# A softmax attention whose second query chunk takes its steps on the diagonal between its full steps

## The chip, the cores and the metric

The kernel runs on one core of a Trainium2 chip. The metric is the time of one execution on the device in microseconds. Five engines work side by side, each through its own list of instructions in order: TensorE (PE, with its weight loads as PEld), VectorE (DVE), ScalarE (ACT), GpSimd (POOL) and SyncE (SP, which issues DMAs). They meet only at semaphores.

## What is computed

Two transformer layers over x of 2 sequences, 1024 tokens and 256 channels. Layer 0 is a polynomial attention of 16 heads and an expert layer with two experts. Layer 1, cut to what matters here, is a causal softmax attention of 32 heads of width 8, followed by an expert layer with 32 experts:

```python
scores = jnp.einsum('bhqd,bhkd->bhqk', q, k) / math.sqrt(dh)
causal = jnp.tril(jnp.ones((T, T), dtype=bool))
scores = jnp.where(causal[None, None], scores, -jnp.inf)
weights = jax.nn.softmax(scores, axis=-1)
out = jnp.einsum('bhqk,bhkd->bhqd', weights, v)
```

Nothing outside this softmax attention is touched.

## The kernel before, in words

The softmax attention works through 16 quads, G = 0 to 15: four heads of one sequence each, eight quads per sequence. A planner (`plan_second_attention`) writes the order of the work once; every engine then takes its own part of it in that order.

A quad has two chunks of 512 queries. `key_steps(c)` (line 308) lists the steps of chunk c; a step is one block of 128 keys, or two such blocks packed into one width:

- chunk 0: step 0 is key block 0, 512 queries wide; step 1 packs key blocks 3 (128 wide) and 1 (384 wide); step 2 is key block 2, 256 wide. All three lie on the diagonal.
- chunk 1: steps 0 to 3 are key blocks 0 to 3, each 512 wide and wholly under the diagonal ("full"). Step 4 is key block 4, 512 wide, on the diagonal; step 5 packs key blocks 7 (128) and 5 (384); step 6 is key block 6, 256 wide.

So a quad has ten steps, and each step has two halves of two heads. One half is, in PE's order (`weights`, line 1175, and `weigh`, line 1152):

1. in quads 8 to 15 (`KEPT_BUSY`), one matmul of constants that is never read (`keep_busy`, L2450);
2. the scores of two heads (`scores`, L2436), into a pair of PSUM banks;
3. beside them a unit of score maxima of the other two heads of the *next* quad (L2408), into two of three single banks. DVE reduces them (L3059 with a mask, L3062 without). A table, `PLAN_OF_STEP`, says at which of the ten places n = 0 to 9 such a unit stands; only n = 5 has none. The last quad has none at all;
4. one part of a `weigh` (L2461): the products of the softmax weights with v, accumulated in one bank. They belong to the step two places earlier (`weigh_due`, line 1170, with `WEIGHTS_AHEAD = 2`). A full step has two parts of 256 columns; step 5 has parts of 384 and 128; step 6 has two parts of 128. At the first places of a quad they are held back and then come three in a row.

ACT takes the exponentials of each half (L2790), 1024 elements per partition, or 512 for a 256-wide step. For a step on the diagonal POOL then clears the forbidden triangle (`mask_weights`, L3716), once for each key block of the step, and the weigh of that step waits for it. After the last weigh of a chunk ("closes") ACT copies the bank out (L2709, `o_cols`).

Other work stands at fractional places in a list called `between`. For every quad: `cut_max` and `turn_max` of the second half at 0 and 2 (POOL's copies L367 and L3673, PE's transposes L2347, ACT's copy to `qt`); `normalize` of the previous quad at 2.5 (PE transposes the output, DVE takes the reciprocal at L3088 and multiplies at L3091 into `ao`, which frees a pair of banks); `cut` of quad G + 2 on POOL at 3.5 (at 4.2 in quad 6); `turn` of quad G + 2 at 7.2. In quads 5 and 6 the projection of the second sequence runs in between, in quads 8 and 9 a `norm` of four tiles stands at place 6 and 4 (POOL, L3681 to L3707), and from quad 13 on POOL issues scatter DMAs for the next layer.

The order of the ten steps before is chunk 0, steps 0 to 2, then chunk 1, steps 0 to 6. The loop that walks them is line 1328:

```python
for n, (c, step) in enumerate((c, step) for c in range(SEQ // QCH) for step in range(len(key_steps(c)))):
    half_steps = weights(G, c, step, beside[2 * n:2 * n + 2])
```

Of the kernel before, what the change touches and what calls it, by code (L numbers as in the profile page):

```python
# [17 lines left out]
BATCH, SEQ, CH = 2, 1024, 256  # L18
# [5 lines left out]
QCH = 512  # L24
# [283 lines left out]
def key_steps(c):  # L308


    d = 4 * c
    return [([(key, 0)], QCH) for key in range(d + 1)] + [([(d + 3, 3 * P), (d + 1, 0)], QCH), ([(d + 2, 0)], 2 * P)]
# [5 lines left out]

RAISED_ON_ACT = ((1, 1, 2), (1, 2, 2), (1, 3, 0))
MIXED_STEPS = ((0, 0), (1, 0), (0, 1), (0, 2), (1, 1), (1, 4), (1, 5), (1, 2), (1, 6), (1, 3))  # L320


CUT_PLACES = (((2.5, 3, 3.5, 4, 5, 7.5), (4.5, 5, 7.6, 7.7, 8, 9.9)), ((0, 1, 2, 2.0, 4, 6.5), (4, 4.5, 6.6, 6.7, 7.5, 9.5)))
# [46 lines left out]
def build_program(nc, ins, out):  # L370
    ctx = ExitStack()
    with ctx:
# [115 lines left out]
        def walk(work_of):  # L488
# [501 lines left out]
            def plan_second_attention(A, start, late, w_ready, during, tail, amid):  # L990
# [160 lines left out]
                def weigh():  # L1151
                    G, c, step, part, slot, ready = due.pop(0)
                    b, quad = divmod(G, quads)
                    bank_free = o_free[0] if step == 0 and part == 0 else ()
                    done = mark(weighed, L, b, quad, c, step, part)
                    if part:
                        probs_ring.give(slot, done)
                    closes, oc, oc_free = part and step == len(key_steps(c)) - 1, None, ()
                    out_open[0] = None if closes else False
                    if closes:  # L1160
                        if c == 0:
                            o_turn[G] = (*oc_ring.take(), [])
                        oc, oc_free = o_turn[G][0:2]
                        o_out = mark(act_copied, "o", L, b, quad, c)
                        o_turn[G][2].append(o_out)
                        o_free[0] = (o_out,)
                    do("weigh", A=A, b=b, quad=quad, c=c, step=step, part=part, slot=slot, waits=(*ready, *bank_free),
                       first=step == 0 and part == 0, closes=closes, oc=oc, oc_free=oc_free)
# [6 lines left out]
                def weights(G, c, step, maxima):  # L1175
                    b, quad = divmod(G, quads)
                    keys, _ = key_steps(c)[step]
                    p_slot, p_free = probs_ring.take()
                    ready = []
                    for h0 in (0, 2):  # L1180
                        slot, slot_free = pairs.take()
                        q_slot, _, q_ready = qt_at["max", G]
                        k_slot, _, k_ready = kt_at[G]
                        gone = mark(scored, L, b, quad, c, step, h0)
                        done = mark(exped, L, b, quad, c, step, h0)
                        pairs.give(slot, done)
                        ready.append(done)
                        if c == 1 and step == len(key_steps(c)) - 1 and h0:
                            kt_ring.give(k_slot, gone)
                            max_ring.give(q_slot, gone)  # L1190
                        units = maxima[h0 // 2]
                        if G in KEPT_BUSY:
                            keep_busy(1)
                        do("scores", A=A, b=b, quad=quad, c=c, step=step, h0=h0, p_slot=p_slot, p_free=p_free, slot=slot,
                           slot_free=slot_free, q_slot=2 + q_slot, k_slot=k_slot, rows_ready=(q_ready[c], *k_ready),
                           qk_done=(), on_act=False, before=start, maxima=max_places(*units[0]) if units else None)
                        for unit in units[1:]:
                            max_unit(unit[0], unit[1:])
                        weigh_due(h0 // 2)
                        if h0 == 0:  # L1200
                            yield
                    if keys[0][0] >= 4 * c:
                        for key, _ in keys:
                            masked = mark(pool_raised, L, b, quad, c, step, "masked", key)
                        do("mask_weights", A=A, b=b, quad=quad, c=c, step=step, p_slot=p_slot, ready=tuple(ready))
                        ready = [masked]
                    due.extend((G, c, step, part, p_slot, tuple(ready)) for part in range(2))
# [78 lines left out]
                for G in range(last + 1):  # L1286
                    b, quad = divmod(G, quads)
                    between = list(during(b, quad))
                    beside = [[] for _ in range(2 * len(PLAN_OF_STEP))]
                    if G == 0:  # L1290
                        for n, unit in enumerate(max_units(LATER_PLANS)):
                            beside[n // 2].append((0, *unit))
                        for n, unit in enumerate(max_units()):
                            beside[6 + (n // 2 if n < 8 else n - 4)].append((1, *unit))
                        between += [(1.5, lambda: turn(1)), (2.8, lambda: cut_max(0, 1)), (2.9, lambda: turn_max(0, 1)),
                                    (5, lambda: cut_max(1, 0)), (8, lambda: turn_max(1, 0)), (0.5, scales[0]), (1.4, scales[1])]
                    else:
                        between += [(0, lambda: cut_max(G, 1)), (2, lambda: turn_max(G, 1))]
                    if 0 < G < last:
                        for n, plan in enumerate(PLAN_OF_STEP):  # L1300
                            if plan is not None:
                                for half in range(2):
                                    beside[2 * n + half].append((G + 1, plan, 2 - 2 * half))
                        between += [(2.8, lambda: cut_max(G + 1, 0)), (5, lambda: turn_max(G + 1, 0))]
                    if G + 2 <= last:
                        at = {quads - 3: 2.6, quads - 2: 4.2}.get(G, 3.5)
                        between += [(at, lambda: cut(G + 2)), (7.2, lambda: turn(G + 2))]
                    if quad:
                        between.append((2.5, lambda: normalize(G - 1)))
                    elif b:  # L1310
                        between += [(1, lambda: normalize_half(0, 1)), (2, lambda: turn_out(0, 1, 0)), (2.8, lambda: turn_out(0, 1, 1)),
                                    (3.8, lambda: project_out(0, 1)),
                                    (6, norm)]
                    if (b, quad) == (1, 1):
                        between.append((4, norm))
                    if G == quads - 3:
                        between += [(1.2 + 1.1 * n, lambda n=n: bring_half_x(1, n // 2, n % 2)) for n in range(4)]
                        between += [(5.4 + 0.9 * t, lambda t=t: project(1, t)) for t in range(5)]
                    if G == quads - 2:
                        between += [(0.6 + 1.1 * (t - 5), lambda t=t: project(1, t)) for t in range(5, TILES)]  # L1320
                    if quad == quads - 1:
                        between += [(5, lambda: normalize_half(1, 0)), (5.8, lambda: turn_out(1, 0, 0)), (6.2, lambda: turn_out(1, 0, 1)),
                                    (7, lambda: project_out(1, 0)),
                                    (7.1, lambda: early.extend(plan_norm(norms_due.pop(0)))), (7.5, lambda: early[0]()),
                                    (9, lambda: early[1]()), (9.1, lambda: early[2]())] if b else [
                                    (5.5, lambda: normalize_half(0, 0)), (6.8, lambda: turn_out(0, 0, 0)), (7.6, lambda: turn_out(0, 0, 1)), (8.5, lambda: project_out(0, 0))]
                    between.sort(key=lambda p: p[0])
                    for n, (c, step) in enumerate((c, step) for c in range(SEQ // QCH) for step in range(len(key_steps(c)))):
                        half_steps = weights(G, c, step, beside[2 * n:2 * n + 2])
                        for at in (n, n + 0.5):  # L1330
                            while between and between[0][0] <= at:
                                between.pop(0)[1]()
                            next(half_steps, None)
                    for _, what in between:
                        what()
# [2537 lines left out]
```

How the kernel before makes its waits and increments, by code:

```python
    def wait_ge(self, signal, *name):  # L83
        value = signal.at[name]
        if self.reached.get(signal.sem, 0) < value:
            self.eng.wait_ge(signal.sem, value)
            self.reached[signal.sem] = value
# [2139 lines left out]
            def attention_weights(A, free):  # L2227
                L = A.layer
                for e in free:
                    q.wait_ge(*e)
                load(f"wqkv{L}", stage[:, 0:KB * 3 * CH].rearrange("p (k n) -> p k n", k=KB),
                     ins[f"wqkv{L}"].rearrange("(k p) n -> p k n", p=P))
                load(f"wo{L}", stage[:, KB * 3 * CH:KB * 4 * CH].rearrange("p (k n) -> p k n", k=KB),
                     ins[f"wo{L}"].rearrange("(k p) n -> p k n", p=P))
                if L == 0:
                    load_x(1)
# [1 line left out]
            def attention_setup(A, start):  # L2238
                L = A.layer
                for e in start:
                    q.wait_ge(*e)
                load(f"cos{L}", A.cos[:], ins[f"cos{L}"])
                load(f"sin{L}", A.sin[:], ins[f"sin{L}"])
                if not A.softmax:
                    load("qk_scale", A.qk_scale[:], ins["ln_scale"].partition_broadcast(P))
                    load("qk_bias", A.qk_bias[:], ins["ln_bias"].partition_broadcast(P))
# [8 lines left out]
            def many_setup(start):  # L2255
                for e in start:
                    q.wait_ge(*e)
                load(f"gw{ml}", M.gw[:], ins["router1"].rearrange("(k p) n -> p k n", p=P))
```

## Time and profile before

| what | us |
| --- | --- |
| median of 3 runs | 1542.97 |
| lowest, highest | 1540.48, 1550.19 |
| the profiled execution's own time | 1543.04 |
| its span, from the first to the last instruction | 1541.3 |
| the softmax attention in it, first to last exponential | 645.7 to 1246.4 |

The span is what the rows of the trace add up to; about 1.7 us lie outside it. Rows of a timeline give start and duration in us, and in brackets the idle time of the engine just before and what ended it. TensorE's clock is given as the share of full speed that was granted: 1.00 is 2.4 GHz, 0.50 is 1.2 GHz.

### The profile page before, as it was taken

The page shows a single profiled execution, that of the slowest core. Times are in us where ns is not written, and L with a number is a line of the kernel's source. Part 1 is how long each engine was busy: PE and PEld are TensorE (multiplying, and loading weights), DVE is VectorE, ACT ScalarE, POOL GpSimd, SP SyncE. Part 2 cuts the span into 40 slices and gives each one's busy share as a digit, 9 for nine tenths or more (in the row PEclk, how much of TensorE's full clock was granted, in tenths as well). Part 3 has the DMA queues.
Part 4 walks back from the last instruction along what each step waited for, and adds up shares of the span by engine and source line. Part 5 has one row for each costly group of instructions (what it writes and reads, how often), then busy time and mean ns, then how long its engine had stood idle before and what let it go on. Part 6 is the DMA issues. An engine that isn't in the chain of part 4 may idle for free.

```text
span 1541.3 us, 26468 instructions
## 1 busy us (share of the span) xinstructions
PE 1305.7 (85%) x9434; PEld 827.6 (54%) x9434; DVE 1041.7 (68%) x2748; ACT 880.1 (57%) x1245; POOL 681.1 (44%) x862
## 2 busy tenths in 40 slices
PE   6477756776789999689999998999999988899995
PEld 4233443342567877444544554434444454899984
DVE  7757787768444365878877477767997366555685
ACT  3578626877343342347777566666667652466660
POOL 7477254647202103313232741442237637766661
PEclk9599986988999999769999989979999979999999
DMA  2690000012302101000000000000004435677876
GB/s 95 217 362 29 1 1 1 1 42 99 110 11 72 42 11 36 11 1 1 2 1 1 1 1 1 1 2 1 1 2 159 175 148 198 216 210 215 265 259 225
DMA packets 69143, 124.40 MB, mean 81 GB/s; under 512 B 7318, under 2 KB 55190, under 8 KB 67992
## 3 DMA queue, kind: packets, MB, share of 16 engines
q1 hardware_dynamic: 56728, 85.99, 17.2%
q0 software_dynamic: 12288, 36.72, 6.4%
q8 instruction: 80, 1.31, 0.3%
q14 instruction: 47, 0.39, 0.1%
HBM read 60.29 MB, written 62.39 MB: 80 GB/s over the span
## 4 chain that ended last, share of the span: by engine, by line
PE 54%; DVE 25%; ACT 11%; POOL 4%; issue 4%; DMA 2%; SPq 0%; POOLq 0%; DVEq 0%; ACTq 0%
PE psum L2461 10%; PE psum L2347 8%; PE psum L2436 6%; PE psum L2667 6%; DVE psum L3059 5%; PE psum L2566 4%; DVE probs L3079 4%; ACT probs L2792 3%; PE psum L2690 3%; PE psum L2408 3%; PE psum L2587 3%; PE psum L362 2%; PE psum L2450 2%; DVE neg_max L3062 2%; PE psum L2368 2%
## 5 line engine op out<-in xcount | busy, mean ns | idle before, releaser
L2790 ACT ACTIVATE probs<-psum,exp_shift 128x1024 f32<-128x1024 f32 (+1 forms) x320 | 325.8, 1032 | 148.7 <-PE psum L2436 144.2
L3059 DVE CUSTOM_DVE_ANT_0 psum<-psum,stage 128x512 f32<-128x512 f32 (+3 forms) x512 | 288.6, 618 | 86.4 <-PE psum L2408 86.2
L3716 POOL TENSOR_SCALAR_AFFINE_SELECT probs<-probs 128x512 f32<-128x512 f32 x192 | 139.8, 740 | 370.9 <-ACT probs L2790 266.3
L2436 PE MATMUL psum<-qt,kt 32*128 32x512 f32 (+5 forms) x1152 | 240.7, 452 | 51.7 <-ACT probs L2792 18.8
L2408 PE MATMUL psum<-kt,qt 32*128 32x512 f32 (+3 forms) x768 | 209.3, 456 | 20.8 <-DVE neg_max L3059 14.4
L3079 DVE TENSOR_TENSOR probs<-probs 128x1024 f32<-128x1024 f32 (+1 forms) x136 | 170.2, 1296 | 61.6 <-ACT probs L2792 61.3
L2436 PEld LDWEIGHTS psum<-qt,kt 32*128 32x128 f32 (+1 forms) x1152 | 106.7, 197 | 193.7 <-issue 75.1
L2461 PE MATMUL psum<-probs,v 128*32 128x256 f32 (+3 forms) x2048 | 178.2, 447 | 1.9 <-POOL probs L3716 1.9
L3787 POOL DMA_INDIRECT results<-sp_y,sp_row x128 | 126.1, 985 | 57.4 <-ACT sp_y L2851 29.2
L2792 ACT ACTIVATE probs<-psum 128x1024 f32<-128x1024 f32 (+1 forms) x160 | 140.2, 946 | 5.8 <-PE psum L2436 5.8
L3062 DVE TENSOR_REDUCE neg_max<-psum 128x1 f32<-128x256 f32 (+3 forms) x256 | 111.1, 484 | 29.8 <-PE psum L2408 29.5
L2408 PEld LDWEIGHTS psum<-kt,qt 32*128 32x128 f32 x768 | 97.4, 198 | 51.4 <-DVE neg_max L3059 32.3
L3780 POOL DMA_INDIRECT many_x<-rows,where x96 | 93.0, 969 | 56.3 <-issue 19.5
L2347 PE MATMUL psum<-ident,q_rows 128*128 128x128 f32 x384 | 65.7, 313 | 52.5 <-ACT k_rows L2709 26.6
L2461 PE MATMUL psum<-probs,stage 128*32 128x256 f32 (+2 forms) x1280 | 99.9, 398 | 0.0
L2566 PE MATMUL psum<-sp_w,sp_xt 128*128 x512 | 95.2, 329 | 1.9 <-ACT sp_y L2851 1.0
L2566 PEld LDWEIGHTS psum<-sp_w,sp_xt 128*128 128x128 f32 x512 | 87.2, 192 | 6.9 <-issue 3.9
L2347 PEld LDWEIGHTS psum<-ident,q_rows 128*128 128x128 f32 x384 | 47.1, 157 | 75.8 <-DVE q_rows L3036 36.6
L2461 PEld LDWEIGHTS psum<-probs,v 128*32 128x32 f32 x2048 | 48.9, 114 | 65.8 <-issue 49.5
L2709 ACT ACTIVATE qt<-psum 128x512 fp32r<-128x512 f32 (+1 forms) x69 | 52.7, 764 | 44.0 <-PE psum L2347 43.9
L3059 DVE DVE_READ_ACCUMULATOR2_ANT neg_max<- 128x1 f32 x512 | 72.5, 142 | 0.0
L3513 DVE TENSOR_TENSOR shid<-psum,ssilu 128x512 f32<-128x512 f32 x36 | 24.9, 692 | 68.7 <-PE psum L2667 63.4
(362 smaller groups left out, 2587.0 us busy)
## 6 DMA issues: line engine op xcount, KB each, us to landing
many_x<-blank SPq DMA_DIRECT2D x2, 10240.0 KB, 50.6
sp_xs<-many_x SPq DMA_DIRECT2D x64, 320.0 KB, 3.8
sp_w<-in_sparse SPq DMA_DIRECT2D x8, 1280.0 KB, 9.2
x_turned<-results SPq DMA_DIRECT2D x8, 768.0 KB, 7.2
sp_back<-results SPq DMA_DIRECT2D x8, 768.0 KB, 10.5
sorted_x<-blank SPq DMA_DIRECT2D x2, 1152.0 KB, 6.5
sorted_y<-y SPq DMA_DIRECT2D x18, 128.0 KB, 1.7
rows<-in_x SPq DMA_DIRECT2D x4, 512.0 KB, 6.9
```

The costliest lines, as they stand in the source:

```text
L2347: inst = pe.transpose(dst[:, i * P:(i + 1) * P], tile, ident[:])
L2408: scored_max[i] = pe.matmul(psum[:, base:base + (k1 - k0) * P], A.qt[rows, q_slot, tile * P:(tile + 1) * P], A.kt[rows, k_slot, k0 * P:k1 ...
L2436: inst = pe.matmul(psum[:, base - early:base + QCH - q0], A.kt[rows, k_slot, key * P:(key + 1) * P], A.qt[rows, q_slot, c * QCH + q0 - ear ...
L2461: inst = pe.matmul(psum[32 * h:32 * h + 32, bank + q0:bank + q1], A.v_of(b)[:, key, col:col + 32], A.probs[:, slot, h, at:at + q1 - q0], s ...
L2566: inst = pe.matmul(psum[:, at:at + GATED], M.xt[:, x_slot, n * CH + k * P:n * CH + (k + 1) * P], M.w[:, bass.ds(which[2 * p + n], 1), k * ...
L2790: inst = act.activation(dst, view, ACT.Exp, bias=exp_shift[:, 0:1])
L2792: inst = act.activation(dst, view, ACT.Square)
L3059: inst = dve.tensor_tensor_reduce(src, src, causal_bf[:, (4 - cols) * P:4 * P], -1.0, -MASKED, ALU.add, ALU.min, dst)
L3062: inst = dve.tensor_reduce(dst, src, X_AXIS, ALU.max, negate=True)
L3079: dve.tensor_tensor(dst, dst, dst, ALU.mult).then_inc(raised.by(A.layer, b, quad, c, step, h0), 1)
L3716: pool.affine_select(out=dst, in_=dst, compare_op=ALU.is_ge, fill=0.0, base=0, pattern=[[0, 4], [1, P]], channel_multiplier=-1).then_inc(p ...
L3787: pool.indirect_dma_start(results, bass.IndirectOffsetOnAxis(M.row[:, row_slot, n:n + 1], 0), M.y[:, y_slot, n * CH:(n + 1) * CH], None).t ...
```

## The change

The ten steps of a quad are taken from a table in which chunk 1 alternates: 0, 4, 1, 5, 2, 6, 3. "The last step of a chunk", which decides when the output bank is closed and when the buffers of a quad are given back, now comes from the same table.

```diff
+EVEN_STEPS = ((0, 0), (0, 1), (0, 2), (1, 0), (1, 4), (1, 1), (1, 5), (1, 2), (1, 6), (1, 3))
+LAST_STEP = {c: [step for chunk, step in EVEN_STEPS if chunk == c][-1] for c in range(SEQ // QCH)}
...
-                    closes, oc, oc_free = part and step == len(key_steps(c)) - 1, None, ()
+                    closes, oc, oc_free = part and step == LAST_STEP[c], None, ()
...
-                        if c == 1 and step == len(key_steps(c)) - 1 and h0:
+                        if c == 1 and step == LAST_STEP[c] and h0:
...
-                    for n, (c, step) in enumerate((c, step) for c in range(SEQ // QCH) for step in range(len(key_steps(c)))):
+                    for n, (c, step) in enumerate(EVEN_STEPS):
```

The units of maxima and the list `between` go by the place n and stay where they are. What stands at the places is:

| n | 0 | 1 | 2 | 3 | 4 | 5 | 6 | 7 | 8 | 9 |
| --- | --- | --- | --- | --- | --- | --- | --- | --- | --- | --- |
| before | 0.0 | 0.1 | 0.2 | 1.0 | 1.1 | 1.2 | 1.3 | 1.4 | 1.5 | 1.6 |
| after | 0.0 | 0.1 | 0.2 | 1.0 | 1.4 | 1.1 | 1.5 | 1.2 | 1.6 | 1.3 |

All line numbers below line 330 are four higher in the changed kernel.

TensorE, from place n = 9 of one quad to n = 1 of the next (here quads 2 and 3), before. L2436 are scores, L2408 maxima, L2461 weighs, L2347 the transposes of `turn_max`:

```order
L2436 MATMUL psum<-qt,kt 128x256 x2
L2408 MATMUL psum<-kt,qt 128x512 x2
L2461 MATMUL psum<-probs,v 32x256 x4
L2436 MATMUL psum<-qt,kt 128x512 x2
L2408 MATMUL psum<-kt,qt 128x512 x2
L2461 MATMUL psum<-probs,v 32x384 x4
...
L2436 MATMUL psum<-qt,kt 128x384 x2
L2408 MATMUL psum<-kt,qt 128x128 x2
L2408 MATMUL psum<-kt,qt 128x384 x2
L2461 MATMUL psum<-probs,v 32x128 x4
L2347 MATMUL psum<-ident,q_rows 128x128 x4
```

and now:

```order
L2440 MATMUL psum<-qt,kt 128x512 x2
L2412 MATMUL psum<-kt,qt 128x512 x2
L2465 MATMUL psum<-probs,v 32x256 x4
L2440 MATMUL psum<-qt,kt 128x512 x2
L2412 MATMUL psum<-kt,qt 128x512 x2
L2465 MATMUL psum<-probs,v 32x128 x4
...
L2440 MATMUL psum<-qt,kt 128x384 x2
L2412 MATMUL psum<-kt,qt 128x128 x2
L2412 MATMUL psum<-kt,qt 128x384 x2
L2465 MATMUL psum<-probs,v 32x256 x4
L2351 MATMUL psum<-ident,q_rows 128x128 x4
```

The scores at n = 9 went from 256 to 512 columns, the first weigh of the next quad from 384 to 128, and the two weighs at n = 1, the second of which closes the chunk, from 128 to 256.

GpSimd in quad 8, from the last copy of `cut` over the `norm` to the next `cut_max`, before. L3716 are masks, L3681 to L3707 the `norm`:

```order
L367 TENSOR_SCALAR k_rows<-qk 128x32x8
L3681 TENSOR_TENSOR ln_stats<-ln_sd,ln_rstd 128x4
...
L3707 TENSOR_SCALAR rows<-rows,ln_mean_var,ln_rstd 128x256 x4
L3716 AFFINE_SELECT probs<-probs 128x4x128 x4
L367 TENSOR_SCALAR q_rows<-neg_max 128x16
```

and now:

```order
L371 TENSOR_SCALAR k_rows<-qk 128x32x8
L3720 AFFINE_SELECT probs<-probs 128x4x128
L3685 TENSOR_TENSOR ln_stats<-ln_sd,ln_rstd 128x4
...
L3711 TENSOR_SCALAR rows<-rows,ln_mean_var,ln_rstd 128x256 x4
L3720 AFFINE_SELECT probs<-probs 128x4x128 x3
L371 TENSOR_SCALAR q_rows<-neg_max 128x16
```

One mask went ahead of the `norm`. The number of masks is the same; the first of the three behind the `norm` is now that of place n = 6 and no longer that of n = 8.

## Rows read from the trace of the kernel before

**Rows 1.** groups by form: count | busy us, mean ns | idle

```profile
L2790 ACT ACTIVATE probs<-psum,exp_shift 128x1024 f32<-128x1024 f32 x256 | 281.9, 1118 | 115.2 <-PE psum L2436 111.5
...
L3059 DVE CUSTOM_DVE_ANT_0 psum<-psum,stage 128x512 f32<-128x512 f32 x316 | 209.7, 721 | 79.5 <-PE psum L2408 79.3
...
L3716 POOL TENSOR_SCALAR_AFFINE_SELECT probs<-probs 128x512 f32<-128x512 f32 x128 | 80.2, 639 | 266.6 <-ACT probs L2790 266.3
...
L2450 PE MATMUL psum<-stage 128*128 128x512 bf16 x126 | 50.9, 404 | 0.0
...
L2790 ACT ACTIVATE probs<-psum,exp_shift 128x512 f32<-128x512 f32 x64 | 43.9, 688 | 33.5 <-PE psum L2436 32.7
```

**Rows 2.** windows: PE PEld DVE ACT POOL, clock; quads 1-4, 1-15

```profile
701.60:731.50 29.90, 28.61 (x292) 14.10 (x288) 24.98 (x85) 23.56 (x27) 9.78 (x25) 1.00 0.01 1
731.50:761.30 29.80, 28.50 (x292) 14.11 (x288) 24.92 (x83) 23.56 (x27) 9.16 (x19) 1.00 0.01 2
761.30:794.60 33.30, 32.78 (x292) 16.03 (x288) 25.27 (x84) 23.79 (x27) 9.15 (x19) 0.85 0.01 1
794.60:824.40 29.80, 28.49 (x292) 14.10 (x288) 24.92 (x83) 23.57 (x27) 9.16 (x19) 1.00 0.00 1
701.60:1246.00 544.40, 511.37 (x4654) 250.82 (x4647) 394.30 (x1294) 375.88 (x423) 219.34 (x380) 0.94 0.07 26
```

**Rows 3.** timeline, TensorE, quad 2, places 0, 1, 3 and 5

```profile
731.27 0.85 PE L2461 MATMUL psum<-probs,v 128*32 128x384 f32 x8
...
732.06 0.49 PE L2436 MATMUL psum<-qt,kt 32*128 32x512 f32 x2
...
735.56 0.42 PE L2461 MATMUL psum<-probs,v 128*32 128x128 f32 x8
...
735.91 0.66 PE L2347 MATMUL psum<-ident,q_rows 128*128 128x128 f32 x4
...
739.39 0.50 PE L2436 MATMUL psum<-qt,kt 32*128 32x512 f32 x2 [0.54 <-DVE ao L3091]
...
747.67 0.64 PE L2461 MATMUL psum<-probs,v 128*32 128x256 f32 x8
...
748.24 0.50 PE L2436 MATMUL psum<-qt,kt 32*128 32x512 f32 x2
```

**Rows 4.** timeline, VectorE, quad 2: normalize, and the maxima after place 7

```profile
738.53 0.35 DVE L3088 RECIPROCAL o_rcp<-psum 128x32 f32<-128x32 f32 x1
...
754.69 0.70 DVE L3059 CUSTOM_DVE_ANT_0 psum<-psum,stage 128x512 f32<-128x512 f32 x1 [1.88 <-PE psum L2408]
```

**Rows 5.** windows around half-clock stretches, quads 3 and 7

```profile
761.30:765.80 4.50, 4.48 (x52) 2.02 (x44) 4.48 (x20) 3.83 (x4) 1.09 (x3) 0.98 0.00 0
765.80:775.80 10.00, 9.77 (x60) 5.14 (x56) 6.20 (x24) 3.76 (x6) 5.01 (x11) 0.50 0.00 0
915.80:926.00 10.20, 9.97 (x66) 5.21 (x64) 6.69 (x26) 4.37 (x6) 4.53 (x11) 0.50 0.01 2
```

**Rows 6.** timeline, GpSimd (quads 2, 6, 8, 9), then TensorE (quads 6, 8, 9)

```profile
744.86 0.41 POOL L367 TENSOR_SCALAR k_rows<-qk 128x256 fp32r<-128x256 f32 x1
...
899.22 0.41 POOL L367 TENSOR_SCALAR k_rows<-qk 128x256 fp32r<-128x256 f32 x1
...
982.30 4.86 POOL L3707 TENSOR_SCALAR rows<-rows,ln_mean_var,ln_rstd 128x256 f32<-128x256 f32 x4
...
1013.37 4.85 POOL L3707 TENSOR_SCALAR rows<-rows,ln_mean_var,ln_rstd 128x256 f32<-128x256 f32 x4
...
899.16 0.64 PE L2461 MATMUL psum<-probs,v 128*32 128x256 f32 x8
...
986.96 0.64 PE L2461 MATMUL psum<-probs,stage 128*32 128x256 f32 x8
...
1018.43 1.08 PE L2461 MATMUL psum<-probs,stage 128*32 128x256 f32 x8
```

**Rows 7.** timeline, ScalarE, last exponential of quad 15

```profile
1245.74 0.69 ACT L2790 ACTIVATE probs<-psum,exp_shift 128x512 f32<-128x512 f32 x1
```

## The prediction

> **What bounds the kernel now.** Only the softmax attention changes, so I read that stretch. First the groups by form [rows 1], for what one instruction costs. A unit of maxima is two reductions of 512 columns; DVE gives 209.7 us to 316 of them, 0.66 us each, so a unit takes 1.33 us. An exponential of a half takes ACT 1.12 us, or 0.69 us where the step is 256 wide; a mask takes POOL 0.64 us.
>
> Second the busy time in windows of one quad [rows 2]. Quads 1, 2 and 4 take 29.8 to 29.9 us each at a clock of 1.00. In 29.8 us PE is busy 28.5, DVE 24.9, ACT 23.6, POOL 9.2. No engine is full: PE's busy time holds its waits for banks inside matmuls, and DVE is idle for 29.8 - 24.9 = 4.9 us. Quad 3 does the same work, 292 matmuls, in 33.3 us at a clock of 0.85. That is the largest difference between equal quads, and this change could touch it.
>
> Third the timelines of PE and DVE in quad 2. Start to start, a weigh of 384 columns takes PE 732.06 - 731.27 = 0.79 us, one of 128 takes 735.91 - 735.56 = 0.35, one of 256 takes 748.24 - 747.67 = 0.57 [rows 3]. Scores with maxima beside them take about 0.43 us (the matmul of 0.50 without its tail). So a full half costs PE 0.43 + 0.57 = 1.0 us against DVE's 1.33: wherever maxima stand in a row, DVE sets the pace. It waits for PE where PE does other things: the row at 754.69 has DVE idle for 1.88 us behind the transposes of place 7 [rows 4]. From there DVE works on to place 3 of the next quad, where PE waits for DVE's `ao` [rows 3, 4].
>
> **The change part by part.** It adds and removes no instruction and no DMA. Ten steps keep ten places; the steps on the diagonal of chunk 1 move from places 7, 8, 9 to 4, 6, 8, and each weigh follows two places later. The sum of the work of each engine is the same, so only what it meets counts.
>
> 1. *Weighs, quads 1 to 7.* The weighs at the eight halves of n = 8, 9, 0, 1 were 256, 256, 256, 256, 384, 128, 128, 128. They become 384, 128, 256, 256, 128, 128, 256, 256. At n = 8 PE then needs 0.43 + 0.79 = 1.22 us, still under DVE's 1.33: nothing. At n = 1 each weigh costs 0.57 - 0.35 = 0.22 us more. The first stands before a wait for a bank of DVE and is lost in it. The second pushes the transposes at 735.91, ACT's copy and `normalize`, whose reciprocal at 738.53 DVE reaches with next to nothing to spare [rows 4], and PE waits for its product at 739.39 [rows 3]. I take half of 0.22, 0.1 us. The packed step at n = 6 costs PE 0.05 us more ahead of maxima. 0.15 x 7 = +1.0 us (bounds 0 and 0.22 x 7 = 1.5).
>
> 2. *Weighs, quads 8 to 14.* Here each half has one more matmul, of 0.40 us with its tail [rows 1] and some 0.32 without. The first half of n = 0 took PE 0.32 + 0.43 + 0.79 = 1.54 us, over DVE's 1.33; it now takes 1.1, and n = 1 with 1.32 stays under DVE's longer units of 128 and 384 there. The gain is at most 1.54 - 1.33 = 0.2 a quad. I take 0.15: -1.0 us (bounds 0 and -1.5).
>
> 3. *Masks behind other work on POOL.* A mask now stands at n = 4, behind `cut`, and its weigh is due at n = 6. In most quads the mask has room: in quad 2 `cut` ends at 744.86 + 0.41 = 745.27 [rows 6], and the weigh stands 0.43 us behind the scores of 748.24 [rows 3]. Three places are tight [rows 6]. Quad 6: `cut` ends at 899.22 + 0.41 = 899.63, the mask 0.64 and a hand-over later at 900.35; the weigh stood at 899.16: 1.2 us late. Quad 8: the `norm` ends at 982.30 + 4.86 = 987.16, the two masks of n = 6 at 988.4; the weigh at n = 8 stood at 986.96: 1.4 us late. Quad 9: the `norm` ends at 1018.22, the mask at 1018.95; the weigh stood at 1018.43: 0.5 us. Queued behind the weigh on PE are the next scores and maxima, for which ACT and DVE wait. The sum is 3.1 us if nothing hides it, 0 if DVE's backlog hides all of it; there is little backlog at n = 6, so I take 3.1.
>
> 4. *The end.* The last step of quad 15 had an exponential of 0.69 us (at 1245.74) [rows 7], a mask of 0.64 and two weighs of 128; now two exponentials of 1.12, no mask and two weighs of 256. ACT gains one short exponential at n = 8 and gives two at n = 9: +0.43; the closing weighs +0.44; the mask ended just ahead of its weigh and frees some 0.2. +0.7 us (bounds 0 and +1.3, all of it exposed).
>
> 5. *The clock.* In quad 3 the clock fell to half (1.2 GHz) from 765.8 to 775.8 [rows 5]; in quad 7 from 915.8 to 926.0, at the same place of the quad, from the end of n = 1 to n = 4. Before the first fall PE had not been idle (4.48 of 4.50 us busy), but had just done the three weighs of 128 columns in a row, with the narrow maxima of n = 1. These are the weighs that the change makes 256 wide. The price of a fall is 33.3 - 29.8 = 3.5 us [rows 2]. If the thin work brought the clock down, both go: -7.0 us. The other falls in the stretch (0.06 x 544.4 x 2 = 65 us at half clock in all, 20 of them these two) I leave. Bounds: 0, and 65 x 0.35 = -23, all gone at 3.5 us per 10. I take -7.0, since the row right before the fall is the one that changes.
>
> The Trainium skill ("TensorE: Matmul & The Clock Gate", section "HAM oscillation — how this bites in real kernels") speaks against term 5: it lays a fall of the clock to gaps in which the engine stands idle. The row before the fall shows no such gap. By that rule the change would give no clock back, and the sum would be 7 us higher, which is the first rival.
>
> Sum on the span of 1541.3: +1.0 - 1.0 + 3.1 + 0.7 - 7.0 = -3.2, so 1538.1; with the 1.7 us outside it 1539.8. The profiled execution took 1543.04 and the median is 1542.97, so this stands for the median too. About 1% (15 us) is what a measurement of this kernel can tell from no change.
>
> **The rivals.**
>
> *The clock stays as it is.* The falls do not hang on the width of two weighs. For it: quads 1, 2 and 4 have the same thin weighs and no fall. Against: two falls at one place. Time: 1539.8 + 7.0 = 1546.8.
>
> *Slower: the thin place only moves.* At n = 8 to n = 0 the weighs were 256, 256, 256, 256, 384, 128 and are 384, 128, 256, 256, 128, 128: four thin halves where there was one. If the clock falls there in the plain quads 1 to 7, each costs 3.5 us. All seven: 1546.8 + 24.5 = 1571. It decides over 1% from the fourth fall: 1546.8 + 14 = 1561, over 1558.4. For it: POOL's and PE's new waits in quads 6, 8 and 9 add idle time too. Against: scores are 512 wide at n = 9 now and not 256, and n = 1 is fuller by 0.44 us.
>
> *Faster: the clock stays up nearly everywhere.* More even weighs keep it up in the other quads as well. Time: 1546.8 - 23 = 1524. For it: term 5 claims less than a third of the 65 us at half clock. Against: nothing in the change touches the other waits of the stretch.
>
> *It does nothing.* Terms 1 to 5 within a microsecond or two, 1543; it lies inside the first two cases and has no chance of its own.
>
> **How the numbers follow.** My case 0.5 (from 1535 to 1544), the clock stays 0.28 (1543 to 1551), the thin place moves 0.10 (three in four of it over 1558), the clock stays up 0.12 (most of it under 1527.5). Faster by over 1%: 0.11. Slower by over 1%: 0.07. Within 1%: 0.82. The range leaves out the far ends of the last two cases: 1527 to 1554.
>
> **What would show it.** Right: 29.9 to 30.1 us for quads 1 to 4 each, quad 3 among them, with a clock of 1.00; the first weigh after place 6 in quad 6 and after place 8 in quad 8 with an idle time of over 1 us put to the masks (POOL); the last chunk closed within 1 us of before, against the start of quad 15. Wrong: a quad 3 at 33 us, or falls in quads 1, 2 or 4 between n = 8 and n = 1; DVE idle inside n = 8 to n = 3; PE waiting for masks in quads where I have them early. If a plain quad at full clock is over 0.5 us longer or shorter than 29.8, terms 1 and 2 are wrong, and the time follows that, sixteen times.

## The result, and the profile after

The changed kernel takes 1550.78 us (median of 20 runs, 1542.23 to 1574.58) beside 1542.83 of the kernel before (20 runs, 1532.48 to 1550.57). The ratio is 1.005, with a 95% interval of 1.0029 to 1.0072: 7.7 us slower by the ratio (8.0 between the medians), where 3 us faster was forecast. The runs spread more than before: 11 of the 20 are over 1550 us. The time goes with the clock: the two runs at a mean clock of 0.914 took 1543.0 and 1543.2 us, the three at 0.904 took 1551.4 to 1559.1. The profile caught a short run (1544.30 us, span 1542.5, clock 0.913), so it shows what the change costs at a good clock, and not the whole loss. Every ratio leaves out the runs that are over 1.5% above the fastest of their kernel, and the tables of profiles leave out two such runs (e3 and e15).

The windows of the quads after, to be held against [rows 2], from a quad's first exponential to the next one's (quads 1 to 5, 8, 9, 14, 15, then 1 to 15). The columns are as there: length, busy PE, PEld, DVE, ACT, POOL, then the clock:

```profile
701.60:732.90 31.30, 29.67 (x289) 14.13 (x288) 25.43 (x85) 23.76 (x27) 9.15 (x19) 0.95 0.00 1
732.90:764.60 31.70, 30.12 (x289) 14.21 (x288) 25.10 (x84) 23.60 (x27) 9.14 (x19) 0.95 0.01 2
764.60:794.60 30.00, 28.45 (x289) 13.91 (x288) 25.04 (x84) 23.55 (x26) 9.16 (x19) 1.00 0.00 1
794.60:824.70 30.10, 28.53 (x289) 13.89 (x288) 25.13 (x84) 23.62 (x27) 9.16 (x19) 1.00 0.00 1
824.70:876.00 51.30, 46.51 (x377) 26.58 (x376) 28.42 (x88) 30.01 (x40) 25.74 (x38) 0.90 0.00 1
954.30:997.30 43.00, 39.67 (x342) 19.96 (x340) 30.01 (x98) 25.43 (x28) 16.04 (x33) 0.88 0.00 1
997.30:1037.70 40.40, 36.22 (x309) 15.89 (x311) 27.68 (x95) 24.27 (x26) 16.03 (x33) 0.83 0.00 1
1176.00:1206.10 30.10, 28.73 (x290) 12.46 (x294) 25.50 (x85) 22.27 (x25) 23.44 (x30) 1.00 0.51 187
1206.10:1245.80 39.70, 36.75 (x292) 17.81 (x291) 10.20 (x35) 28.39 (x31) 23.91 (x29) 1.00 0.46 166
701.60:1245.80 544.20, 506.86 (x4654) 248.11 (x4654) 394.21 (x1296) 374.80 (x422) 219.16 (x375) 0.95 0.07 26
```

Quads 3 and 4 at a clock of 1.00 take 30.0 and 30.1 us, where quads 2 and 4 took 29.8. The fall of quad 3 is gone, as forecast. But quads 1 and 2 now each have a short stretch at half clock (0.95), quad 5 has 0.90 where it had none, and quad 8 has 0.88 where it had 0.96; quad 9 is low in both (0.83, and 0.79 before). Over all, the clock is 0.95 beside 0.94 and the 15 quads take 544.2 us beside 544.4. What was given back in one place was taken in another.

The waits for masks came where step 3 put them (TensorE's timeline in quads 6, 8 and 9, to be held against [rows 6]; behind the bracket is the idle time before the row and what ended it):

```profile
904.22 0.64 PE L2465 MATMUL psum<-probs,v 128*32 128x256 f32 x8 [1.10 <-POOL probs L3720]
...
991.68 0.85 PE L2465 MATMUL psum<-probs,stage 128*32 128x384 f32 x8 [1.25 <-POOL probs L3720]
...
1021.52 1.08 PE L2465 MATMUL psum<-probs,stage 128*32 128x256 f32 x8 [1.17 <-POOL probs L3720]
```

1.10 + 1.25 + 1.17 = 3.5 us, 3.1 forecast (1.2, 1.4 and 0.5: the one of quad 9 is twice what was taken). Of the weighs, the two rows that moved most are in TensorE's timeline at n = 0 and 1 of quad 3:

```profile
765.84 0.50 PE L2412 MATMUL psum<-kt,qt 32*128 32x512 f32 x1 [0.24 <-DVE neg_max L3063]
...
767.62 0.64 PE L2465 MATMUL psum<-probs,v 128*32 128x256 f32 x8
```

The first is a maxima matmul that waits 0.24 us for a bank of DVE (in quad 2 of before the pair at this place, from 732.06, took 0.81 us and had its wait inside); the second a weigh of 256 columns where [rows 3] has one of 128. And at the end, the transposes of `ranks` wait 2.41 us for ACT and waited 1.99.

### The profile page after: what moved, and what is told of

Same layout as the page of the kernel before. It is cut to its first block, busy times and chain, and to the rows that moved or that the text cites. A ratio compares the mean times of both kernels' runs of the same rounds, so it can differ in the third digit from the quotient of the medians.

```text
span 1542.5 us, 26467 instructions
## 1 busy us (share of the span) xinstructions
PE 1305.4 (85%) x9434; PEld 828.1 (54%) x9434; DVE 1041.4 (68%) x2748; ACT 879.1 (57%) x1245; POOL 681.0 (44%) x862
## 3 DMA queue, kind: packets, MB, share of 16 engines
q1 hardware_dynamic: 56728, 85.99, 17.1%
## 4 chain that ended last, share of the span: by engine, by line
PE 50%; DVE 26%; ACT 11%; POOL 5%; issue 4%; DMA 3%; SPq 0%; POOLq 0%; DVEq 0%; ACTq 0%
PE psum L2465 9%; PE psum L2351 8%; DVE psum L3063 7%; PE psum L2671 6%; PE psum L2440 5%; PE psum L2570 4%; DVE probs L3083 4%; ACT probs L2796 3%; PE psum L2694 3%; PE psum L2412 3%; PE psum L2591 3%; PE psum L366 2%; DVE neg_max L3066 2%; PE psum L2454 2%; PE psum L2372 2%
## 5 line engine op out<-in xcount | busy, mean ns | idle before, releaser
L3791 POOL DMA_INDIRECT results<-sp_y,sp_row x128 | 126.0, 984 | 55.8 <-ACT sp_y L2855 26.9
```

The lines of the kernel that those rows point to most:

```text
L3791: pool.indirect_dma_start(results, bass.IndirectOffsetOnAxis(M.row[:, row_slot, n:n + 1], 0), M.y[:, y_slot, n * CH:(n + 1) * CH], None).t ...
```

## The experiments

Each was timed in 5 rounds (e5 in 2) beside runs of the kernel before on the same chip, and the ratios are to those. Beside the first twelve the kernel before takes 1622.7 to 1624.6 us ("the 1623 runs"), beside the last six 1543.1 to 1544.5, as in the case. What makes the difference is not known: the record has chip 15 in both groups. The longer time lies from quad 14 on, where the scatter DMAs run: from the start of the last exponential 368 us remain in e1's profile and 297 in the one above. Quads 1 to 13 take the same in both groups. All edits but e5's stand on the changed kernel; a table says for each quad which order it takes:

```diff
+PLAIN_STEPS = ((0, 0), (0, 1), (0, 2), (1, 0), (1, 1), (1, 2), (1, 3), (1, 4), (1, 5), (1, 6))
+STEPS_OF = [EVEN_STEPS if G in (...) else PLAIN_STEPS for G in range(16)]
```

"New order" is EVEN_STEPS and "old order" PLAIN_STEPS.

**e1**, the changed kernel once more.

> The changed kernel once more, unchanged, to see whether a profile of its longer runs differs from the one at 1544.3 us by the clock alone. If the loss is made of falls of the clock, the median is again 5 to 9 us over the kernel before, the runs spread over 15 us or more, and a run's span follows its mean clock: over 1550 us at 0.905 and below, about 1543 at 0.912 and above. If it is made of fixed work (waits for masks, wider weighs), the runs spread no more than those of the kernel before (10 us or so) at one clock.

1.0111 (1.0071 to 1.015), 18 us, where 5 to 9 were expected. Clock against time holds: one run took 1652.2 us at 0.879, another 1627.9 at 0.898, and the runs spread over 30 us. Its quads 1 to 13 agree with those of the profile above to 0.1 us each, falls included.

**e2, e3, e4**: the change in three parts.

> The new order in quads 0 to 5 alone. Theory C (the thin place between n = 8 and n = 0 brings the clock down in the plain quads, which have no keep_busy): most of the loss is here, +5 to +8 us, with half-clock stretches in quads 1, 2 and 5. Theory M (the loss is in the places where PE waits for a mask): none of these is here, so +0 to +1.5 us (0.3 a quad) minus up to 3.5 for the fall of quad 3, so -2 to +1.5.

> The new order only in quads 6, 8 and 9, where PE waits for masks. Theory M: the waits of 1.10, 1.25 and 1.17 us and the clock that they cost are here: +4 to +8 us, with a half-clock stretch in each of quads 8 and 9. Theory C: the waits alone, +3 to +3.5 us, and the clock as before.

> The new order in quads 7 and 10 to 15. These have keep_busy (but for quad 7) and no mask that is late. Both theories: +0 to +1 us from the end of quad 15 and -0 to -3.5 from the fall of quad 7, so -3 to +1; the clock as in the kernel before. More than +3 here would break both and leave the order's own cost in the busy quads.

1.0024 (0.9992 to 1.0056), 1.004 (1.0001 to 1.0078) and 1.0078 (1.004 to 1.0115). The largest part is the one in which neither theory had a loss, so both are broken there. E2 and e3 decide nothing: 3.9 and 6.5 us, each with an interval of 5 to 6 us either way. E4's profile and e1's differ from the others in the last quads. E1 first, quads 14 and 15:

```profile
1179.60:1216.00 36.40, 30.82 (x285) 13.32 (x294) 25.93 (x86) 22.45 (x24) 24.75 (x33) 0.92 0.44 161
1216.00:1271.40 55.40, 52.44 (x288) 25.06 (x293) 10.08 (x32) 28.59 (x31) 22.37 (x26) 0.62 0.32 115
```

The clock falls at 1213.6, just ahead of quad 15, and stays at half for 44.4 us. Some 3 us before it, DVE starts a reduction 1.5 us after its matmul has ended, and PE stands still behind it (DVE's timeline, then TensorE's):

```profile
1210.85 0.70 DVE L3063 CUSTOM_DVE_ANT_0 psum<-psum,stage 128x512 f32<-128x512 f32 x1 [1.63 <-PE psum L2412]
```

```profile
1211.66 0.49 PE L2412 MATMUL psum<-kt,qt 32*128 32x512 f32 x1 [1.18 <-issue]
```

**e5**: the kernel before, unchanged, in the first group.

> The kernel before, unchanged, for a profile from the same chip as the runs beside it. If the loss of the changed kernel on the longer runs sits in its last quads (a stretch at half clock of 44 to 58 us from quad 14 on, seen in the two earlier runs with the new order there), this one has there less than 30 us at half clock; if it is the chip and not the order, it has as much.

0.9989 (0.9957 to 1.0021): no difference, as it must be. Quads 1, 2 and 15:

```profile
704.70:735.80 31.10, 30.07 (x289) 15.19 (x288) 25.37 (x85) 23.73 (x26) 10.14 (x28) 0.95 0.00 1
735.80:769.10 33.30, 32.77 (x289) 16.04 (x288) 25.25 (x84) 23.79 (x26) 9.15 (x20) 0.85 0.01 2
1209.50:1263.20 53.70, 49.75 (x288) 23.32 (x286) 11.34 (x33) 28.98 (x32) 23.40 (x29) 0.68 0.35 121
```

34.1 us at half clock in quad 15, 41 with quad 14: neither "less than 30" nor quite "as much". It begins 16 us into quad 15 and not before it. The first two rows tell more: in this execution of the same kernel the long fall is in quad 2, and quad 3 takes 29.9 us at 1.00. In which quad a fall stands is no property of the quad.

**e6, e7**: `KEPT_BUSY = tuple(range(1, 16))`, with the old and the new order.

> The old order with keep_busy in quads 1 to 15 in place of 8 to 15. Quads 1, 2 and 4 at full clock stay within 1 us of 29.8. Theory C (thin PE work before the fall): the falls of quads 3, 5 and 7 go, 3.5 us each: -5 to -14 us. If keep_busy costs more than it gives: 0 to +7.

> The new order with keep_busy in quads 1 to 15. Theory C (the loss of the new order is its thin place in the quads without keep_busy): this is within 3 us of e6, the old order with the same keep_busy. Theory M (masks that are late in quads 6, 8 and 9) or a loss in the last quads: it stays 5 to 15 us longer than e6.

1.008 (1.0044 to 1.0116) and 1.0156 (1.0121 to 1.0192). Quad 1 of e6:

```profile
706.70:738.30 31.60, 29.25 (x304) 14.03 (x309) 25.53 (x85) 24.12 (x26) 9.82 (x26) 1.00 0.00 1
```

The mean clock rises (0.898 in e6's runs, 0.894 beside them), but every plain quad pays 1.8 us at full clock, while a fall costs 3.5 in about one plain quad of four. E7 is 0.76% of the time behind e6, 12 us, which theory C excluded.

**e8**: the new order, with the mask ahead of what it waited for.

```diff
-                        at = {quads - 3: 2.6, quads - 2: 4.2}.get(G, 3.5)
+                        at = {quads - 3: 2.6, quads - 2: 4.6}.get(G, 3.5)
...
-                                    (6, norm)]
+                                    (6.6, norm)]
...
-                        between.append((4, norm))
+                        between.append((4.6, norm))
```

> The new order, with the norms of quads 8 and 9 and the cut of quad 6 moved half a step later, behind the mask that stood behind them. The waits of PE for masks in quads 6, 8 and 9 (1.10, 1.25, 1.17 us) go. Theory M: 4 to 8 us less than the changed kernel, quads 8 and 9 near 39.8 and 40.1 us as before. Theory C or a loss in the last quads: 3.5 us less and no more, still 5 us or more over the kernel before.

1.0041 (1.0 to 1.0082), where e1 had 1.0111: 11 us less, known to about 9. Quads 8 and 9:

```profile
959.50:999.30 39.80, 35.94 (x329) 18.98 (x334) 29.62 (x95) 25.53 (x29) 15.39 (x32) 0.96 0.01 1
999.30:1032.60 33.30, 29.43 (x305) 14.09 (x308) 27.77 (x94) 24.02 (x26) 16.48 (x34) 1.00 0.00 1
```

Together 73.1 us, and 83.4 in e1. PE's waits for masks in quads 6 to 9 fell to 1.5 us, from the 3.5 above; the rest of the ten is clock, 1.00 in quad 9 and not 0.83. Theory M has its 4 to 8 us and more in size. Its mechanism is not borne out: in the profile after, the falls of quads 8 and 9 begin 6.4 and 18.0 us into them (at 960.7 and 1015.3), and PE's waits for masks in these quads end later, at 991.7 and 1021.5. What brings those falls on, and why they go when the `norm` moves, isn't shown.

**e9, e10**: the new order in all quads but 14, and in 14 alone.

> The new order in every quad but 14, whose last weighs stand at the start of quad 15. Theory L (the loss is that the clock falls at the start of quad 15 and not 17 us later in it, because quad 14 ends thinner in the new order): the half-clock stretch in quad 15 begins 15 to 18 us after its first exponential, quads 14 and 15 together take 79 to 88 us and not 92 to 97, and the kernel is 6 to 10 us under the changed kernel of the same chips (about 1.005 times the kernel before). Theory S (the loss is spread over all quads): under 2 us less than the changed kernel.

> The new order in quad 14 alone. Theory L: +6 to +10 us over the kernel before, with a stretch at half clock that begins within 3 us of quad 15's first exponential; quads 1 to 13 as before. Theory S: under +1.5 us.

1.0035 (0.9993 to 1.0076) and 1.005 (1.0025 to 1.0076): theory L in both, for the 1623 runs. Quads 14 and 15 of e10:

```profile
1177.60:1214.80 37.20, 31.15 (x285) 13.55 (x294) 25.83 (x86) 22.31 (x25) 25.37 (x34) 0.89 0.42 156
1214.80:1273.00 58.20, 54.56 (x287) 25.27 (x290) 10.46 (x32) 29.20 (x31) 22.07 (x27) 0.60 0.30 111
```

95.4 us, and in e9 79.0. Over the profiles of the 1623 runs, the two last quads took 91.8, 97.1, 93.3, 91.8, 95.4 and 93.2 us with the new order in quad 14 (e1, e4, e7, e8, e10, e11) and 78.8, 87.7, 86.1, 79.0 and 82.2 with the old one (e2, e5, e6, e9, e12).

**e11**: PE filled around the start of quad 15.

```diff
-                            keep_busy(1)
+                            keep_busy(2 if (G, c, step) in ((14, 1, 6), (14, 1, 3), (15, 0, 0)) else 1)
```

> The new order in all quads, with keep_busy doubled in the last two steps of quad 14 and the first of quad 15: six more matmuls of constants, some 0.32 us each, 1.9 us at most. If the fall at the start of quad 15 comes from the thin weighs there, it goes, and quad 15 is 6 to 9 us shorter at a cost of 1 or 2: 5 to 8 us under the changed kernel. If it comes from the 1.2 us that PE stands idle just before it (DVE starts a reduction late in quad 14, seen in the runs of the new order there), it stays and the kernel is 1 to 2 us longer.

1.0111 (1.0064 to 1.0157). The fall at the start of quad 15 went (the first steps take 2.5, 3.3, 2.8 us and not 3.8, 4.9, 3.9), but this execution had 17.1 us at half clock in quad 14, ahead of the filled place, and lost there as much. That it would have had them without the filling isn't shown.

**e12**: e8 with the old order in quad 14.

> The best of the new order: as e8 (norms and cut behind the masks), with the old order in quad 14. Theory L with the masks: both losses go, so 1612 to 1628 us beside 1623 of the kernel before, a ratio of 0.994 to 1.003. If another cost of the new order is left, over 1.004.

1.0068 (1.0033 to 1.0103): missed. The two mends do not add. Its profile is of the shortest of its twelve runs; quads 8 and 9 take 73.2 us in it, as in e8's.

**e13**: the old order with e8's places of the norms (`(6.6, norm)`, `(4.6, norm)`).

> The old order with the norms of quads 8 and 9 half a step later, as in e8. If the 6 us that quads 8 and 9 were shorter in the profiles of e8 and e12 (73.2 us against 79.9) come from where the norms stand: quads 8 and 9 at 73 to 76 us and the kernel 4 to 7 us under the kernel before, 0.996 to 0.997. If they come from the order with the norms behind the masks: 79 to 82 us, no change or up to 3 us longer, since the norm now stands ahead of the mask of n = 7.

1.0024 (0.9994 to 1.0054), quads 8 and 9 at 79.1 us, the second case: in this one profile the places are worth nothing to the old order, where no mask stood behind the norm.

**e14, e15, e16**: another order, with three full steps last, in quad 14 of the old kernel; in quad 14 of e8; and everywhere, with both norms at 6.6 and the cut at 4.6.

```diff
+EVEN_STEPS = ((0, 0), (0, 1), (0, 2), (1, 0), (1, 4), (1, 5), (1, 6), (1, 1), (1, 2), (1, 3))
```

> The old order, and in quad 14 alone the diagonal steps early and three full ones last (0, 4, 5, 6, 1, 2, 3), so that all weighs from n = 9 on, the first four of quad 15 among them, are 256 wide. Thin weighs as the cause: no fall at the start of quad 15; quads 14 and 15 at 79 to 88 us, as with the old order; the kernel within 3 us of the one before. A late start of DVE as the cause (or any change of quad 14's order): the fall stays, 92 to 97 us, and 6 to 10 us over the kernel before.

> The new order with the norms and cut behind the masks (as e8) and quad 14 with its full steps last (as e14). If the two losses are all there is: 0.996 to 1.003 of the kernel before. If the new order costs also in the plain quads: 1.004 to 1.008, as e12.

> All quads with 0, 4, 5, 6, 1, 2, 3, the norms of quads 8 and 9 at place 6.6 and the cut of quad 6 at 4.6. Narrow scores stand at n = 5 and 6 and the thin weighs at n = 7 and 8, where the maxima are full. Thin weighs as what brings the clock down: quads 1 to 4 near 30 us each, no fall at a quad's start, and the kernel no slower than the one before (0.994 to 1.002). If it is any shift of work that makes new falls: 1.003 to 1.012.

1.0011 (0.9971 to 1.0051), 1.0052 (1.0021 to 1.0083) and 0.9978 (0.9948 to 1.0008). E14's runs fall into five of 1538 to 1546 us and seven of 1556 to 1565; the ratio has only three of the seven in it, and over all twelve the median is 1557.1 beside 1544.5. So "within 3 us" holds for the ratio alone. E15 is in its second case, as e12 was. E14's profile is from a long run; quad 15:

```profile
1204.80:1257.20 52.40, 48.67 (x288) 23.04 (x290) 10.68 (x35) 28.95 (x32) 23.17 (x28) 0.71 0.35 126
```

No fall at its start, as the thin weighs would have it, but 30.7 us at half clock from 17 us on. A long run can be quad 15 alone.

E16 is no slower than the kernel before, as its case of thin weighs had it, but its plain quads are not "near 30 us each". They are 32.5, 33.2, 32.0 and 32.9 us, longer than in any other profile together. The first two, and the fall at the end of the second:

```profile
703.80:736.30 32.50, 30.86 (x292) 13.66 (x292) 25.66 (x83) 23.56 (x27) 8.94 (x19) 0.87 0.00 1
736.30:769.50 33.20, 31.80 (x292) 14.06 (x296) 25.51 (x83) 23.71 (x26) 9.12 (x20) 0.86 0.01 2
...
766.40:776.60 10.20, 10.20 (x79) 3.73 (x72) 8.77 (x33) 6.49 (x7) 1.47 (x4) 0.50 0.01 3
```

**e17, e18**: `(5.5, lambda: normalize_half(1, 0))` in place of 5 in quad 15, in the changed kernel and in e16.

> The changed kernel with the first normalize of quad 15's own output moved half a step (from 5 to 5.5), so that PE has the scores of another half to do while ACT copies the bank that it waited 1.18 us for. If that idle time is what lets the clock stay at half in the rest of quad 15: the long runs go, the spread shrinks to that of the kernel before, and the median is 0.998 to 1.002 of it. If the half clock of quad 15 has another cause (quad 15 has no maxima and PE is thin all through it, or quad 14's end): the long runs stay and the ratio is 1.004 to 1.012.

> e16 (full steps last in every quad, 0.9978 of the kernel before) with the same move in quad 15. If the idle time at place 5 decides: 0.993 to 0.997. If not: as e16, 0.996 to 1.000, or up to 3 us longer, since the projection behind it comes closer to the end.

1.0057 (1.0024 to 1.009) and 0.9958 (0.9929 to 0.9987). Over all its twelve runs e17 has a median of 1556.5 beside 1543.1. Its profile is at last one of a long run of the new order, span 1560.2. The wait of 1.18 us at place 5 of quad 15 (TensorE for ACT's `o_cols`, at 1220.78 in the profile after) is gone in it; one of 0.75 stands at another place. Quads 2, 8 and 15:

```profile
738.30:772.90 34.60, 33.83 (x289) 16.10 (x288) 25.39 (x84) 23.73 (x26) 9.13 (x19) 0.80 0.01 2
967.80:1013.30 45.50, 42.33 (x338) 21.46 (x340) 30.09 (x95) 25.43 (x28) 15.67 (x32) 0.79 0.00 1
1223.60:1262.80 39.20, 36.66 (x292) 17.77 (x288) 10.70 (x35) 28.31 (x32) 23.85 (x29) 1.00 0.46 168
```

Quad 15 is as good as it gets (39.2 us, clock 1.00), and the run is long all the same: the loss is in quads 2, 4, 7, 8 and 13 (34.6, 32.3, 43.3, 45.5 and 36.4 us; in the profile after 31.7, 30.1, 38.1, 43.0 and 34.6). So the wait at place 5 is not what makes long runs.

E18 is under both kernels, 6.5 us under the one before. Its ratio lies among those expected if the idle time at place 5 decides (0.993 to 0.997), but the interval has room for the other case too, and e17 speaks against it. Its quad 1, and quads 2 and 3 take the same 30.3 us:

```profile
705.40:735.70 30.30, 28.80 (x289) 14.01 (x288) 25.13 (x85) 23.56 (x26) 9.11 (x19) 1.00 0.00 1
```

At full clock they are 0.5 us longer than with the old order. What it gains goes with the clock: 0.916 over its runs, 0.911 beside it. Its profile, of a run 10 us above its median, doesn't show where.

## Why the prediction was wrong

**The loss, taken apart.** Quads 1 to 13 take the same in both groups of runs, so every profile that has one order in all of them counts, from the first exponential of quad 1 to that of quad 14:

| order in quads 1 to 13 | us | clock |
| --- | --- | --- |
| old: before, e5, e10, e14 | 472.1, 470.8, 467.8, 470.7 | 0.94, 0.95, 0.95, 0.95 |
| old, norms later: e13 | 475.2 | 0.93 |
| new: after, e1, e11, e9, e17 | 474.4, 474.3, 477.8, 480.1, 485.3 | 0.95, 0.95, 0.93, 0.93, 0.91 |
| new, masks first: e8, e12 | 464.0, 469.2 | 0.96, 0.95 |
| full steps last: e16, e18 | 470.2, 470.8 | 0.94, 0.94 |

The old and the new order do not overlap, over four and five profiles. The means are 470.4 and 478.4: 8.0 us, where 7.7 were measured. That the two agree so well is luck in part: each profile is one run, the new order's spread over 11 us, and quads 0, 14 and 15 are left out. (The two long runs left out of the table have 483.1, e3, with the new order in three quads only, and 474.7, e15, with the masks first.) The mean clock is 0.9475 and 0.934, about 49 and 63 us at half clock; 14 us at 0.35 us each are 4.9 (the price is that of [rows 2, 5]). The other 3.1 are no more than the waits for masks. Profiles at one clock say the same: at 0.95 the new order has 474.4 and 474.3 where the old one has 470.8, 467.8 and 470.7.

Of the 8.0 us, 3.6 are in quad 8 alone, and 2.5 in quads 1 to 4. Quads 8 and 9 together, from first exponential to first exponential, take 79.9, 79.8, 75.8 and 79.8 us with the old order and 83.4, 83.3, 82.7, 80.8 and 84.3 with the new one (in the order of the table). In the 1623 runs the fall around the start of quad 15 comes on top, and the ratio is 1.0111 there.

**Term 1, weighs in quads 1 to 7.** 0.2 to 0.3 us a quad at full clock, 0.15 forecast: right in kind, at the upper bound.

**Term 2, quads 8 to 14.** Wrong in sign. Quad 14 takes 30.1 us at full clock and took 29.8. The first half of n = 0 did get shorter (from 1.56 to 1.17 us, exponential to exponential), but the second took it back (from 1.23 to 1.57), since DVE sets the pace over both. I had counted a saving on PE as one on the path. If quads 8 to 13 are as quad 14, it is 2 to 3 us for the two terms together, and 0 was forecast; with the waits for masks that is more than the 3.1 to 3.6 us that the profiles leave for all fixed costs, so some of it is hidden.

**Term 3, the masks.** Right in place, and in the sum (3.5 us); quad 9 was taken at half. Missed was that these quads also lose clock: e8 took 10 us out of quads 8 and 9 by moving the masks ahead, only 2.0 of them waits for masks. The falls come ahead of the waits (see e8), so the waits are not shown to be their cause.

**Term 4, the end.** Small, as forecast: from the start of the last exponential to the end it is 296.7 us and was 295.6, 1.1 more where 0.7 was the term; 0.4 of it is the wait for `ranks`.

**Term 5, the clock.** This is the step that failed. It said: two falls at one place, so the thin weighs there make them; take them away and the others stay. In the profile after the two falls are gone, but those of quads 1, 2 and 5 are new and that of quad 8 is longer. Quad 3 at 30.0 us was the sign of being right; the fall in quad 1, which begins at n = 1, was the sign of being wrong, and both came. e5 shows why the reading was unsafe: the kernel before, unchanged, has its long fall in quad 2 in another execution, in e10's in quad 4. I had priced single falls from one execution as if they belonged to their quads. What belongs to an order is how much half clock it has on average, and one profile cannot show that.

The other half of the reading, that the thin weighs have to do with it, the runs bear out further than one profile could: the place inside a plain quad is steady and goes with the order. With the old order in quads 1 to 4 (before, e4, e5, e10, e13, e14) the fall of 10.2 us begins 4.6 to 4.8 us into its quad, behind the three weighs of 128 columns at n = 0 and 1. In e9, e11, e12 and e17, with the new order there, the longest fall begins 2.6 to 2.7 us in, behind the weighs of 128 at n = 8 and 0, and lasts 13.7 us. (Falls of 3.4 to 6.8 us begin 2.8 to 3.1 us in, or 9.4 us in, at n = 3.) Quad 2 of e17, up to the fall and in it:

```profile
738.30:740.90 2.60, 2.35 (x28) 1.00 (x27) 2.57 (x10) 2.18 (x2) 0.71 (x3) 1.00 0.00 0
741.00:754.60 13.60, 13.37 (x85) 6.39 (x85) 8.57 (x34) 5.72 (x7) 5.39 (x12) 0.50 0.01 2
```

In e16 the weighs of 128 stand at n = 7 and 8, and the falls at the end of its quads 0, 1, 2 and 4 begin at n = 9. So "take them away" is what failed: the change took no thin weigh away, it moved them, and the falls went along. That the thin weighs are the cause is still argued and not shown: half of the plain quads or more have them and no fall, and no run changed them alone.

**The rivals.** The likeliest case fell with term 5. "The clock stays as it is" (1546.8 us) was the nearest one, and 4 us short. The time lies in the range (1527 to 1554), on the side that I held for the less likely. "The thin place moves" has its mechanism right and its price wrong: the falls moved with the thin weighs, and one in a plain quad is longer in the new order (34.6 us in quad 2 of e17, at 0.80, against 33.3 at 0.85 in [rows 2]). But they are hardly more: two of quads 1 to 4 have one in each profile of the new order, one or two with the old. The price there is 2.5 us on average (126.0 and 123.5), not 14 to 24. Filling those quads with keep_busy (e7) held the clock in three of the four and lost more than it gave. With full steps at the end of the quad e16 and e18 have a clock of 0.914 and 0.916, beside 0.909 and 0.911. That the full steps do it isn't shown: both also have the norms and the cut later, e16's plain quads are the longest of all, and quads 1 to 13 take 470.2 and 470.8 us in their profiles, as in the old order.

The Trainium skill ("TensorE: Matmul & The Clock Gate", section "HAM oscillation — how this bites in real kernels"), which lays falls to gaps in PE's work, was weighed against term 5 in the prediction. By it term 5 would have been 0, and it would have been nearer. The runs do not bear the rule out as the whole cause. For it: in e1, e4, e8 and e10 PE stood still for 1.14 to 1.18 us, and the clock fell at quad 15 about 1 to 2 us later. Against it: in e7 PE stood still for 1.16 us at the same place (to 1224.19) and the clock was at 1.00 for 9.8 us more; in the plain quads PE was busy 4.48 of 4.50 us ahead of the fall in [rows 5] and 2.35 of 2.60 in e17; and taking out the wait of 1.18 us in quad 15 (e17) shortened no long run. A PE that is busy by the profile can be waiting inside a matmul (the pair from 732.06 took 0.81 us where others take 0.50), so short gaps are not excluded.

**What stays open.** Why e12 and e15, which mend both losses, are at 1.0068 and 1.0052 while e8 is at 1.0041: the intervals overlap, and no profile of theirs was taken of a median run. Why DVE starts late at the end of quad 14 in the new order in the 1623 runs (it stands idle for 0.8 to 1.6 us in all six profiles, at most 0.9 with the old order there): the trace names only the matmul that had ended. What brings the falls of quads 8 and 9 on. Which part of e18 (its order, the later norms and cut, the move in quad 15) makes it faster. And how much of the long runs of the changed kernel in the result is quad 15, as in e14, and how much the quads before it, as in e17: none of them has a profile.

## What to carry to other kernels

Where the granted clock changes within a kernel, do not price single falls from one profile: take the kernel's profile twice and see which falls stay. Where a fall stands behind a group of thin steps, ask where the change puts that group: here the falls moved with it and were not given back. A change of order shows in the mean clock over many runs, and in stretches of a dozen tiles, not in one tile. Price the waits it adds (here masks behind a norm) in full. An order that ends each tile with its full steps was the best one here (e18, 0.4% under the kernel before), for reasons that the runs leave open.

## What the runs showed of the hardware

The pattern of falls repeats: the profiles of the changed kernel (the one above and e1's) have quads 1 to 13 equal to 0.1 us, and so have e5 and e14, of the old order, from chips 12 and 13. But one kernel has several such patterns, and they part early: quad 0 in the old order takes 55.5, 57.2, 59.5 and 57.3 us in the four profiles of the table's first row. The Trainium skill says of the clock at a kernel's start that it is "run-variable" ("TensorE: Matmul & The Clock Gate", section "What's actually happening"); here the same holds in the middle of a kernel.

A high clock is no gain by itself: e6 had 0.898 and was 0.8% longer than the kernel before, at 0.894.
